# The last count of a top-k search moved to ScalarE in two of four batches, an earlier pick, one table load, and five new instruction sequences

## What is computed

```python
# graph mixing, h = ctx_512, adj = layernorm(x)
Q, K = (h @ Wq.T), (h @ Wk.T)                      # 4 heads of 32
sim = einsum('bhnd,bhmd->bnm', Q, K) / (sqrt(d) * H)   # [b, 512, 512]
k = int(512 * 0.3)                                 # 153
threshold = top_k(sim, k)[0][:, :, -1:]
A = sigmoid(sim) * (sim >= threshold)
A = (A + A^T) * 0.5
x = x + (1 - gamma) * layernorm(x) + gamma * A
# ternary feed-forward net, F = 2048, rows quantized to 8 bits, weights to -1, 0, 1
z = layernorm(x)
x = x + bitlinear(silu(bitlinear(z, w_gate)) * bitlinear(z, w_up), w_down)
```

## Time and profile before

| | |
|---|---|
| time, median of 3 runs (lowest to highest) | 279.37 us (278.31 to 280.48) |
| the profiled execution's own time | 279.58 us |
| its span, first to last instruction | 277.8 us |
| TensorE, VectorE, ScalarE, GpSimd busy | 79%, 80%, 68%, 61% of the span |
| first gate matmul starts, last down matmul ends | 71.8 us, 274.6 us |

### The profile page before, as it was taken

How to read it: one execution, slowest core, us unless ns; L and a number is a source line. 1 busy time by engine, 2 the same in 40 slices (tenths; PEclk the granted TensorE clock), 3 DMA queues, 4 the chain that set the end, 5 groups by cost and what they waited for, 6 DMA issues and landing times.

```text
span 277.8 us, 3708 instructions
## 1 busy us (share of the span) xinstructions
PE 219.6 (79%) x958; PEld 106.8 (38%) x958; DVE 222.8 (80%) x401; ACT 188.0 (68%) x310; POOL 168.8 (61%) x328
## 2 busy tenths in 40 slices
PE   7803610529679786798997999999999899999985
PEld 7301200418234332333453444344454344444432
DVE  0588887978969999898999998997999758486591
ACT  2498996999988999993547999435547436511420
POOL 2045796867768466798877778896393751420730
PEclk9965595666968999999999999999999999999999
DMA  5999999996355369210805270230503594351758
GB/s 132 396 387 361 268 310 403 308 326 126 64 90 112 68 74 180 51 21 18 116 1 98 54 144 10 58 76 11 90 0 76 165 254 102 33 108 24 154 94 281
DMA packets 78998, 39.18 MB, mean 141 GB/s; under 512 B 67968, under 2 KB 70272, under 8 KB 78464
## 3 DMA queue, kind: packets, MB, share of 16 engines
q1 hardware_dynamic: 78976, 38.94, 56.2%
HBM read 17.96 MB, written 4.19 MB: 80 GB/s over the span
## 4 chain that ended last, share of the span: by engine, by line
PE 29%; POOLq 19%; issue 17%; POOL 15%; DVE 8%; ACT 7%; DMA 4%; DVEq 1%; ACTq 0%
PE DN L404 9%; PE U L385 9%; PE G L371 8%; POOLq L894 4%; POOLq L866 4%; POOL S L955 4%; POOL X L897 4%; POOLq L868 3%; ACT WdT L521 3%; DMA xqT<-qx 2%; POOL srch L869 2%; POOLq L856 2%; POOL sig L849 2%; ACT junk_c L479 1%; ACT S L528 1%
## 5 line engine op out<-in xcount | busy, mean ns | idle before, releaser
L371 PE MATMUL G<-WgT,xqT 128*128 128x512 bf16 x256 | 62.2, 387 | 9.9 <-ACT sg L504 6.5
L504 ACT ACTIVATE sg<-G,gsc 128x1024 f32<-128x1024 f32 x32 | 35.5, 1110 | 43.5 <-PE G L371 36.2
L385 PE MATMUL U<-WuT,xqT 128*128 128x512 bf16 x256 | 60.5, 379 | 0.6 <-DVE S L698 0.5
L698 DVE TENSOR_TENSOR S<-U,sg 128x1024 f32<-128x1024 f32 x32 | 39.1, 1222 | 15.7 <-PE U L385 12.1
L404 PE MATMUL DN<-WdT,S 128*128 128x512 bf16 x208 | 48.0, 379 | 1.4 <-DVE X L757 1.4
L479 ACT ACTIVATE junk_c<-rows,srch 128x512 int8<-128x512 f32 x64 | 45.3, 712 | 4.4 <-POOL srch L859 2.8
L955 POOL TENSOR_SCALAR S<-S,qh 128x2048 int16<-128x2048 f32 x15 | 30.7, 2049 | 22.3 <-DVE qh L747 19.3
L371 PEld LDWEIGHTS G<-WgT,xqT 128*128 128x128 bf16 x256 | 24.6, 99 | 42.8 <-ACT sg L504 6.0
L512 ACT ACTIVATE junk_h<-S 128x2048 int8<-128x2048 f32 x16 | 30.5, 1908 | 10.1 <-DVE S L698 10.0
L385 PEld LDWEIGHTS U<-WuT,xqT 128*128 128x128 bf16 x256 | 24.5, 98 | 32.7 <-DVE S L698 4.3
L703 DVE TENSOR_REDUCE amh<-S 128x1 f32<-128x2048 f32 x15 | 34.0, 2269 | 0.0
...
## 6 DMA issues: line engine op xcount, KB each, us to landing
...
S<-S SPq DMA_TRANSPOSE x17, 4.4
```

The lines of the kernel that those rows point to most:

```text
L371: last = nc.tensor.matmul(G[:, c * 512:(c + 1) * 512], xqT[:, t, k, :], WgT[:, 4 * n:4 * n + 4, k, :], start=(k == 0), stop=(k == KD - 1))
L385: last = nc.tensor.matmul(U[:, c * 512:(c + 1) * 512], xqT[:, t, k, :], WuT[:, 4 * n:4 * n + 4, k, :], start=(k == 0), stop=(k == KD - 1))
L504: A(sg[:, u % 2, :], G[:, :], ACT.Silu, scale=gsc[:, b % 2, t:t + 1]).then_inc(silu_done, 1)
L698: V.tensor_tensor(h[:, i % 2, hs * HF:(hs + 1) * HF], U[:, :], sg[:, u % 2, :], ALU.mult).then_inc(mul_done, 1)
```

## The change

1. In batches 2 and 3 (`ACT_LAST`) the compare pass of `rank` is gone. ScalarE makes a fifth count there (r = 4), whose signs it writes as unsigned bytes, so that -1 becomes 0. `rank_signs` waits for that count of its tile and uses the bytes as the mask: two VectorE passes a tile in place of three. `note_misses` takes the count from `cs`. The bytes must stay until then, so the next batch's first count and first threshold wait for `miss_ready`.
2. `threshold` makes its pick with two operations over all four tiles instead of four, and it now stands ahead of `general_path` in every batch, which repeats the pick in its slow branch (two calls, `h_cast(6)` and `mul(18)`, stand between them in batch 3).
3. `preload_act_table(ACT.Silu)` at the start of ScalarE's list; the compiled program has one table load instead of two.
4. The lists of all five engines are new.

```diff
+    ACT_LAST = (2, 3)
...
+        def rounds_to(a):
+
+            return ROUNDS * a + sum(k < a for k in ACT_LAST)
...
             def counts(a, r, p):
-                act.wait_ge(thr_act, 2 * (ROUNDS * a + r) + p + 1)
+                act.wait_ge(thr_act, 2 * (rounds_to(a) + r) + p + 1)
                 if a and r == 0:
-                    act.wait_ge(cnt_act, NT * ROUNDS * a)
+                    act.wait_ge(cnt_act, NT * rounds_to(a))
+                    if a - 1 in ACT_LAST:
+                        act.wait_ge(miss_ready, a)
                 for j in (2 * p, 2 * p + 1):
-                    A(junk_c[:, j, :], ROWS[a % 2][:, j, :], ACT.Sign, bias=nthr[:, j:j + 1],
+
+                    A(junk_c[:, j, :].bitcast(U8) if r == ROUNDS else junk_c[:, j, :], ROWS[a % 2][:, j, :], ACT.Sign, bias=nthr[:, j:j + 1],
                       accum_out=cs[:, j:j + 1]).then_inc(cnt_act, 1)
...
+            act.preload_act_table(ACT.Silu)
             act.wait_ge(s_small, 48)
...
+            def rank_signs(a, j):
+
+                dve.wait_ge(cnt_act, NT * (rounds_to(a) + ROUNDS) + j + 1)
+                V.scalar_tensor_tensor(mask[:, :], junk_c[:, j, :].bitcast(U8), -BIG, ROWS[a % 2][:, j, :],
+                                       ALU.mult, ALU.add)
+                dve.drain()
+                V.max(m8[:, j, :], mask[:, :])
+                dve.drain()
+
             def rank(a, j):
+                if a in ACT_LAST:
+                    rank_signs(a, j)
+                    return
...
             def note_misses(a):
+                if a in ACT_LAST:
+
+                    V.tensor_scalar(off, cs, 0.5, N / 2 - AIM, ALU.mult, ALU.add)
+                    V.scalar_tensor_tensor(c_fin, m8[:, :, 0], -1.0, nthr, ALU.mult, ALU.is_equal)
+                    dve.drain()
+                    V.tensor_tensor(miss[:, :], off, off, ALU.mult)
+                    dve.drain()
+                    V.scalar_tensor_tensor(miss[:, :], miss[:, :], 16.0, c_fin, ALU.is_gt,
+                                           ALU.max).then_inc(miss_ready, 1)
+                    return
...
             def threshold(a):
 
-                for j in range(NT):
-                    V.scalar_tensor_tensor(pick[:, j, :], place[:, :], off[:, j:j + 1], m8[:, j, :],
-                                           ALU.is_equal, ALU.mult)
+                V.tensor_tensor(pick[:, :, :], place_t, off.unsqueeze(2).to_broadcast([P, NT, 8]), ALU.is_equal)
+                dve.drain()
+                V.tensor_tensor(pick[:, :, :], pick[:, :, :], m8[:, :, :], ALU.mult)
                 dve.drain()
...
             def first_threshold(a, p):
                 js = slice(2 * p, 2 * p + 2)
                 pool.wait_ge(simstat, 2 * a + p + 1)
+                if a - 1 in ACT_LAST:
+                    pool.wait_ge(miss_ready, a)
...
-            c_load(0, 1, 2); w_load(0, w_gate, 0); w_load(0, w_gate, 1); x_load(0); w_load(0, w_gate, 2)
+            w_load(0, w_gate, 0); w_load(0, w_gate, 1); w_load(0, w_gate, 2); c_load(0, 1, 2); c_load(1, 2, 4)
...
-            evac_hT(0); evac_GT(0); sims(0, 0); sims(0, 1); sims(0, 2); sims(0, 3); w_abs(0, 1); counts(0, 0, 0)
+            evac_hT(0); evac_GT(0); w_abs(0, 1); sims(0, 0); sims(0, 1); sims(0, 2); sims(0, 3); evac_hT(1)
```

More of the change, by code:

```diff
@@ L809, in _ @@
-            x_absmax(2, 1); x_absmax(2, 2); x_absmax(2, 3); mul(13); rank(3, 0); x_scale(2, 0, 1, 2, 3)
-            rank(3, 1); mul(14); x_cast(2, 0, 1); h_absmax(6); h_scale(6); mul(15); final(4); x_cast(2, 2, 3)
-            h_absmax(7); h_scale(7); h_cast(6); mul(16); rank(3, 2); final(5); rank(3, 3); note_misses(3); mul(17)
-            general_path(3); threshold(3); h_cast(7); masked(3, 0); mul(18); h_absmax(8); masked(3, 1); mul(19)
-            final(6); h_floor(2); masked(3, 2); masked(3, 3); h_scale(8); h_absmax(9); h_scale(9); mul(20)
@@ L819, in _ @@
[L819 to L820 removed]
+            w_abs(0, 0); sim_stats(0, 0, 1); sim_stats(0, 2, 3); w_abs(0, 2); w_abs(0, 3); x_stats(0, 0, 1)
+            w_scale(0); w_quant(0, 0); w_quant(0, 1); w_quant(0, 2); x_stats(0, 2, 3); rank(0, 0); rank(0, 1)
+            rank(0, 2); rank(0, 3); sim_stats(1, 0, 1); sim_stats(1, 2, 3); note_misses(0); threshold(0)
@@ new lines, in _ @@
+            masked(1, 0); w_scale(2); masked(1, 1); sim_stats(2, 0, 1); mul(0); masked(1, 2); w_quant(2, 0)
+            x_cast(0, 3); masked(1, 3); sim_stats(2, 2, 3); x_stats(2, 0, 1); x_stats(2, 2, 3); mul(1)
+            h_absmax(0); h_floor(0); mul(2); w_quant(2, 1); x1(1, 0); w_quant(2, 2); w_quant(2, 3); mul(3)
+            h_scale(0); h_absmax(1); h_scale(1); x1(1, 1); x1(1, 2); x1(1, 3); mul(4); x_absmax(1, 0); h_cast(0)
+            x_absmax(1, 1); x_absmax(1, 2); x_absmax(1, 3); x_scale(1, 0, 1, 2, 3); mul(5); h_absmax(2)
@@ new lines, in _ @@
+            h_scale(2); h_cast(1); mul(6); x_cast(1, 0, 1); rank(2, 0); rank(2, 1); rank(2, 2); rank(2, 3)
+            note_misses(2); h_cast(2); mul(7); x_cast(1, 2, 3); sim_stats(3, 0, 1); threshold(2); general_path(2)
+            masked(2, 0); mul(8); final(0); masked(2, 1); masked(2, 2); mul(9); sim_stats(3, 2, 3); h_absmax(3)
+            h_scale(3); masked(2, 3); x_stats(3, 0, 1); h_absmax(4); h_floor(1); mul(10); h_cast(3); x1(2, 0)
+            final(1); x1(2, 1); mul(11); x_stats(3, 2, 3); x1(2, 2); final(2); h_scale(4); h_absmax(5); h_scale(5)
@@ new lines, in _ @@
+            x1(2, 3); mul(12); final(3); x_absmax(2, 0); x_absmax(2, 1); h_cast(4); h_cast(5); mul(13)
+            x_absmax(2, 2); x_absmax(2, 3); x_scale(2, 0, 1, 2, 3); mul(14); x_cast(2, 0, 1); h_absmax(6)
+            rank(3, 0); mul(15); final(4); x_cast(2, 2, 3); h_scale(6); h_absmax(7); h_scale(7); rank(3, 1)
+            mul(16); rank(3, 2); rank(3, 3); mul(17); note_misses(3); threshold(3); h_cast(6); mul(18)
+            general_path(3); masked(3, 0); masked(3, 1); mul(19); masked(3, 2); final(5); masked(3, 3)
```

189 lines of the change are left out of this document (92 added, 97 removed).

## The result

The changed kernel takes 272.62 us (median of four runs, 272.46 to 272.84) where the kernel before takes 279.57 us beside it (278.31 to 280.48). The ratio is 0.9761 with an interval of 0.9737 to 0.9786. The forecast was 273.5 us in a range of 269.5 to 279.0.

What follows compares the result with a forecast made beforehand. ScalarE's gapless stretches set `silu(0)` and `silu(7)`; the end is `gate(8)`'s start plus 142.8 us of matmuls plus TensorE's waits. 3.7 us (earlier `gate(8)`) + 2.4 (fewer waits) = 6.1, from 279.58 to 273.5 us, range 269.5 to 279.0.

Steps and rivals of the forecast that it cites:

- The load, 1.3 us: Ahead of `silu(0)` on ScalarE: removing the second table load gives 1.3 us.
- `silu(0)` at 80.8: ScalarE: from 79.46, less 1.3 for the load, plus 2.1 for moved work and 0.5 for a later first search.
- The margin of `x_coef(0)`: On GpSimd, ahead of `silu(0)`: `x_coef(0)` ends near 78, leaving 2.8 us of margin.
- `silu(7)` at 120.7: ScalarE stays gapless from `silu(0)`: new counts add 2.8 us, the 1.75 us of idle time is filled.
- `gate(8)` at 122.0: TensorE: with `down(0)` ahead of `gate(7)`, `gate(8)` starts 3.7 us ahead of 125.74.
- VectorE's rank and `up(8)`: Batch 2's rank ends near 122.7, `mul(7)` near 125.3; `up(8)`, due at 124.9, costs TensorE about half a microsecond.
- Behind `gate(8)`: TensorE's waits there: a walk through the lists finds none of 4.9 us left; half is taken, 2.4 us.
- rival 1: Everything the walk finds comes true: all 4.9 us of waits go, 271.0 us or 269.5; chance 0.18.
- the likeliest case: Half of the waits behind `gate(8)` go; its own range is 271.5 to 276 us, chance 0.51.
- Rival 3: The middle up to `gate(8)` gives nothing, as counts wait for updates: 278.6, from 276.7 to 282 us; chance 0.20.
- rival 4: Slower: batch 3's rows come late for `gate(24)`; decides from a 9 us delay on, 282.5 us or more; chance 0.07.
- Rival 5: A miss flagged in batch 2 or 3 runs the 300 steps, some 900 us; chance 0.01.

Runs made afterwards that it cites:

- a_extra_signs: The changed kernel with each of the four counts of round 1 of batch 2 made twice, a drain between: 275.85 us, ratio 0.9878.
- a_two_loads: The changed kernel without the preload, so the second table load stands again ahead of `silu(0)`: 274.4 us, ratio 0.9844.
- a_signs_3: The changed kernel with ScalarE's fifth count in batch 3 only; in batch 2 VectorE compares as before: 276.4 us, ratio 0.9900.
- a_down_late: The changed kernel with `down(0)` put back behind `gate(7)` and `pre_g(3)`: 273.61 us, ratio 0.9795.
- a_lists_only: The new lists with the code of the kernel before: VectorE's count, two table loads, the old pick: 284.5 us, ratio 1.0160.
- a_vector_counts: The changed kernel with `ACT_LAST` empty and without the eight extra passes, so VectorE compares and counts as before: 280.9 us, ratio 1.0062.
- b_signs: The kernel before with its old lists plus the sign code for batches 2 and 3, no preload, the old pick: 285.1 us, ratio 1.0205.

## Why the prediction was right, point by point

- **What bounds the kernel.** Right up to `silu(5)`: what is added to ScalarE ahead of it is paid one for one (`a_extra_signs`, `a_two_loads`). From there TensorE's own list sets `gate(8)`, and ScalarE's full stretch up to `silu(7)` does not: without the four counts behind `silu(5)` `gate(8)` comes only 0.01 us earlier (`a_signs_3`). The walk through TensorE's list from `gate(6)` on, which gave the term in the sum, had this right. The end is `gate(8)` plus TensorE's work plus its waits.
- **The load, 1.3 us.** Right in size: the row is 1.28 us, `gate(8)` and `gate(31)` move by 1.46 and 1.36, the medians by 1.8, the ratios by 2.3 us. The 2.66 us that the Trainium skill gives (ScalarE: Activation LUTs, What ACT_TABLE_LOAD costs) are not in the trace: in `a_two_loads` the tanh pass ahead starts at 80.00 and lasts 0.62, and the load starts at 80.65, which leaves 0.03 for a drain. What the prediction didn't say is that the gain hangs on the new lists, for in the old ones it is lost in a wait for `gate(1)`.
- **`silu(0)` at 80.8.** It started at 80.50. The first count of batch 1 was late by 0.45 (44.62 against 44.17), priced at 0.5. The margin of `x_coef(0)` was not 2.8 us: it ended at 79.36, 1.1 ahead of `silu(0)`, and not near 78. Against the kernel before its chain on GpSimd started 1.0 us later (75.00 against 73.97), and two of its operations were longer (1.17 and 0.71 us against 1.02 and 0.25). It cost nothing.
- **`silu(7)` at 120.7.** It started at 120.11. ScalarE was gapless, the 1.75 us of idle time went, as said, and the unsigned bytes cost 0.70 a pass like the others.
- **`gate(8)` at 122.0.** It started at 121.56, 4.2 us ahead instead of 3.7. `a_down_late` shows what the earlier `down(0)` gives: 2.6 us at this point, and in the end 1.9 in the traces and 1.0 by the medians.
- **VectorE's rank and `up(8)`.** `mul(7)` ended at 125.24, forecast 125.3, and `up(8)` waited 0.39 us, forecast 0.5.
- **Behind `gate(8)`: the term that was off.** Half of the 4.9 us of waits was to go; 4.3 of the 6.1 us in all went (what stays is the last DMA's 1.1 and 0.7 for `mul`), and the stretch is 3.9 us shorter where 2.4 was in the sum. The walk through the lists was right in finding almost none of them, and the halving for what it can't know was too much. By its mechanism the result is closer to rival 1 (0.18), in which all of them go, than to the half of the likeliest case: rival 1 gives 8.6 us, the traces 8.0, the medians 7.0, and the sum was 6.1. The half was a guess with no row behind it. The experiments also part the two causes that this term took together. With the new lists and without the signs (`a_lists_only`, `a_vector_counts`) TensorE no longer waits for `xqT` or `final` behind `gate(8)`. With the signs in the old lists (`b_signs`) the 1.7 us for `xqT` stay, and it is the wait for `note_misses` that goes. This points to the lists for the 3.1 us of `xqT` and `final`, and not to the compares taken off VectorE. It is not shown beyond doubt, since in the kernels without the signs TensorE is also later there, which can hide such waits.
- **The rivals.** Rival 3, that the middle gives nothing, is excluded by `gate(8)`, 4.2 us earlier, and no count waited for its update, as ScalarE's gapless stretch shows. In rival 4 `gate(24)` started at 214.93 without a wait, where the walk had 213, so the delay was far from the 9 us at which it decides. Rival 5 did not occur, as the time shows.
- **What was not in the prediction.** It took VectorE's relief, 6.6 us, as slack that helps behind `gate(8)`. In the new lists it is a condition: without it the compares come onto the path twice, 8.3 us by the medians. The sum came out near because it priced the lists and the signs together as they stand. Each taken alone was forecast wrong, as the expectations show: near no change where it lost 4 to 6 us.
